# Key and value projection in split float16, and the masks' loads on another queue

## The chip, the cores and the metric

The kernel runs on one core of one Trainium2 chip. The metric is the device time of one execution in microseconds; lower is better. TensorE (PE) multiplies, VectorE (DVE), ScalarE (ACT) and GpSimd (POOL) work on tiles, SyncE (SP) issues transfers. ACT can issue transfers too; what an engine issues stands in its instruction stream, so an engine that waits for a transfer's buffer does nothing else meanwhile.

## The reference

Four blocks, each: cross attention of 256 tokens onto 4096 context rows of width 256 (16 heads of 16), a self-attention-like part, a feed-forward part. Only the context's projections matter here; for every layer l of the four

```
k = context @ Wk[l] + bk[l]      # 4096 x 256
v = context @ Wv[l] + bv[l]      # 4096 x 256
scores = q k^T / 4 (+ mask); out = softmax(scores) (* group_prob in layer 0) v; x = x + out @ Wo + bo
```

The context is the same for the four layers, so the kernel makes all keys and values ahead of the first block.

## The kernel before

`project_context` makes the four layers' keys and values; the rest of the kernel (four times `cross`, and the parts behind it) is not touched. A *key unit* is 128 key channels by 512 keys, 16 for each layer (2 halves of the channels by 8 chunks of the context); a *value unit* is 128 keys by 256 channels, 32 for each layer. The order is written out: the values of layer 0; the keys of layer 0; and for layers 1, 2 and 3 the keys and then the values. Each engine has its own loop over the same units, tied by counting semaphores.

A key unit goes through PE (`key_unit`, L510, two float32 products 128x128 by 512 columns, into one of four PSUM banks), ACT (`high`, L578, writes the float16 high part), DVE (L745, the low part: PSUM plus bias less the high part) and an SP transfer of 256 KB (L469) out of one of five slots of `kp`. The bank is free when DVE is done (`k_low`), the slot when the transfer has landed (`k_stored`). A value unit goes through PE (`value_unit`, L524, two float32 products of 256 columns) and DVE (L631, adds the bias into `vst`); eight units fill one of two slots of `vst`, which SP stores with 1 MB (L458).

While the values of layer 0 are made, the scale of the keys is found: ACT squares all weights (L589), PE sums them (`sum_weights`, L534), DVE reads the context's largest square (L644) and the sums (L652), PE sums again (`sum_squares`, L542), DVE works out a bound (L662 to L672), POOL takes its root (L776), DVE makes the scales, and POOL multiplies `wk` (L780). Then the first key unit can start. After key unit 4's predecessor (`EARLY = 4`) the query of layer 0 is projected in between (L230, L594, L314, L323, L331).

The mask is loaded as 32 pieces of 256 KB into two buffers `raw` (L610) and turned by POOL (L792). ACT issues these loads, eight behind the last key unit of each layer; the one for piece n waits until POOL has made piece n-2. ACT also issues the loads of `gT` (L614), two of 512 KB behind each layer's keys. In layer 2 DVE looks for tokens that see no key (`find_blind`, L711) and SP stores and reloads that row (L475, L462); in layer 3 DVE masks `gT` (`mask_factors`, L732 and L737). Behind the last mask piece POOL multiplies `qop` (L800).

Of the kernel before, what the change touches and what calls it, by code (L numbers as in the profile page):

```python
# [16 lines left out]
P = 128  # L17
D = 256
# [50 lines left out]
EXPONENT = 0x7F800000  # L69

# [303 lines left out]
def project_context(c):  # L374
# [10 lines left out]
    EARLY = 4  # L385
    K_BANKS, V_BANKS = (0, 1, 4, 5), (2, 3, 6, 7)
    X_BANK, Q_BANKS = 2, (3, 6)
    units = [(l, n) for l in range(LAYERS) for n in range(NK)]
    units_by = lambda slot, u: 16 * len([i for i in range(u) if i % VSLOTS == slot])
    stored_by = lambda slot, u: 16 * len([i for i in range(u) if i % SLOTS == slot])  # L390
    with ExitStack() as ctx:
# [3 lines left out]
        ctxT = sb("ctxT", [P, CT, KEYS], F32)  # L395
        wk = sb("wk", [P, LAYERS, CT, D], F32)
        wv = sb("wv", [P, CT, D], F32)
        bk = sb("bk", [P, LAYERS, CT], F32)
        bv = sb("bv", [P, 2, D], F32)
# [3 lines left out]
        wide = lambda first: c.gT[:, first:first + 8, :].rearrange("p (l t) n -> p l t n", l=LAYERS)  # L403
        wq_all, wk_square, wq_square = wide(0), wide(8), wide(16)
        ctx_square = sb("ctx_square", [P, NCHUNK], F32)
        squares = sb("squares", [P, 1 + 2 * LAYERS * CT], F32)
        totals = sb("totals", [P, 1 + 2 * LAYERS * CT], F32)
        quarter = sb("quarter", [P, LAYERS], F32)
        bound = sb("bound", [P, 4, LAYERS], F32)
        factor = sb("factor", [P, 4, LAYERS], F32)  # L410
        k_scale = sb("k_scale", [P, LAYERS], F32)
        per_layer = lambda a, at: a[:, 1 + at * LAYERS * CT:1 + (at + 1) * LAYERS * CT].rearrange("p (l t) -> p l t", l=LAYERS)
        block = ctx.enter_context(nc.Block())
        ctx_v = c.a["ctxT"].rearrange("(t p) k -> p t k", p=P)
        vout = c.vals.rearrange("l p (n h k e) -> l p n h k e", n=NV, h=H, k=VB)

        key_pieces = [m for b in (1, 0) for m in range(KT // 2) if m // 2 % 2 == b]

        def mask_piece(l, i):

            raw_i, n = raw[:, i % 2, :], PIECES * l + i
# [20 lines left out]
        def _(sp):  # L442
            def load_ctx(j):
                sp.dma_start(ctxT[:, :, j * CHUNK:(j + 1) * CHUNK], ctx_v[:, :, j * CHUNK:(j + 1) * CHUNK])\
                  .then_inc(S(f"ctx_loaded{j}"), 16)
# [3 lines left out]
            sp.dma_start(c.bq[:, :, :], c.a["bq4"]).then_inc(S("bias_loaded"), 16)  # L449
            sp.dma_start(c.wq[:, :, :], c.a["wq4"][0, :, :].rearrange("(t p) n -> p t n", p=P)).then_inc(S("wq_loaded"), 16)  # L450
            for j in (4, 1, 5, 2, 6, 3, 7):
                load_ctx(j)
# [12 lines left out]
            for l in range(LAYERS):  # L465
                for n in range(NK):
# [35 lines left out]
        def _(pe):  # L502
            def key_unit(l, n):
                u, mt, j = NK * l + n, n // NCHUNK, n % NCHUNK
                if n == 0:
                    pe.wait_ge(S("wk_scaled"), l + 1)
                if u >= 4:
                    pe.wait_ge(S("k_low"), u - 3)
                for ct in range(CT):
                    ins = pe.matmul(c.ps[:, K_BANKS[u % 4], :], wk[:, l, ct, mt * P:(mt + 1) * P],  # L510
                                    ctxT[:, ct, j * CHUNK:(j + 1) * CHUNK], start=(ct == 0), stop=(ct == CT - 1))
                ins.then_inc(S("k_psum"), 1)

            def value_unit(l, k):
                v = KT * l + k
                if k == 0:
                    pe.wait_ge(S("wv_loaded"), 16 * (l + 1))
# [3 lines left out]
                if l == 0:  # L521
                    pe.wait_ge(S(f"ctx_loaded{at // CHUNK}"), 16)
                for ct in range(CT):
                    ins = pe.matmul(c.ps[:, V_BANKS[v % 4], 0:D], ctxT[:, ct, at:at + P], wv[:, ct, :],  # L524
                                    start=(ct == 0), stop=(ct == CT - 1))
                ins.then_inc(S("v_psum"), 1)

            def sum_weights():
                pe.wait_ge(S("ones_set"), 1)
                pe.wait_ge(S("w_squared"), 2)  # L530
                for square, bank in ((wk_square, 0), (wq_square, 4)):
                    for two in range(2):
                        for ct in range(CT):
                            ins = pe.matmul(c.ps[:, bank + two, :], c.ones[:, 0:P], square[:, 2 * two:2 * two + 2, ct, :],  # L534
                                            start=(ct == 0), stop=(ct == CT - 1))
                ins.then_inc(S("w_summed"), 1)

            def sum_squares():
                pe.wait_ge(S("w_read"), 2)
                pe.wait_ge(S("b_squared"), 2)  # L540
                pe.wait_ge(S("ctx_read"), 1)
                pe.matmul(c.ps[:, 0, 0:1 + 2 * LAYERS * CT], c.ones[:, 0:P], squares[:, :], start=True, stop=True)\  # L542
                  .then_inc(S("squares_summed"), 1)

            for k in range(KT):
                value_unit(0, k)
                if k == 3 * GROUP - 1:
                    sum_weights()
                if k == 7 * GROUP - 1:
                    sum_squares()  # L550
            for l in range(LAYERS):
                for n in range(NK):
                    if NK * l + n == EARLY:
# [6 lines left out]
                        q.project(pe, S, Q_BANKS)  # L560
                    key_unit(l, n)
# [6 lines left out]
        def _(act):  # L568
            def load_values(l):
                act.dma_start(wv[:, :, :], c.a["wv4"][l, :, :].rearrange("(t p) n -> p t n", p=P)).then_inc(S("wv_loaded"), 16)  # L570
# [2369 lines left out]
```

## Time and profile before

| | |
|---|---|
| median of 3 runs | 1500.73 us (1494.08 to 1501.3) |
| the profiled execution: time, span | 1496.89 us, 1495.5 us |
| mean granted clock of TensorE | 0.944 of full |
| busy share of PE, DVE, ACT, POOL | 88%, 67%, 55%, 32% |
| `project_context` | from 0 to 278.5 us of the span |

A time in the trace is counted from the span's start. A matmul of float32 stands in the trace as two instructions. A granted clock of 1.00 is 2.4 GHz, one of 0.50 is 1.2 GHz, and a figure between is a stretch with both.

### The profile page before, as it was taken

To read this page: it belongs to the slowest core of one execution; us is meant where nothing else is said; L and a number is where in the kernel's file an instruction comes from. 1 tells how busy PE (TensorE), PEld (TensorE's weight loads), DVE (VectorE), ACT (ScalarE), POOL (GpSimd) and SP (SyncE) were. 2 spreads that over 40 slices of the span, in tenths; PEclk is the share of its full clock that TensorE was granted. 3 is DMA by queue.
4 is the path that set the end of the run, shared out by engine and by line. 5 is a ranking of instruction groups with operands and counts; after the bars stand their busy time and mean duration, and the time that the engine had idled before them with its cause. 6 is when DMAs were issued, how large, how long until landed. Compare 5 with 4: busy or idle time off the path is not lost. (4 is left out here: it accounts for less than half of the span.)

```text
span 1495.5 us, 29052 instructions
## 1 busy us (share of the span) xinstructions
PE 1319.7 (88%) x10626; PEld 664.7 (44%) x10626; DVE 1006.9 (67%) x2340; ACT 826.4 (55%) x1286; POOL 482.7 (32%) x681
## 2 busy tenths in 40 slices
PE   6879999699999988689999997869999896899987
PEld 4536576333333335523333355424444574344445
DVE  3524647699999944488888424369998144999942
ACT  1122202399999943048888824238888321678872
POOL 1321010489899870334444423111111000111100
PEclk9989999799999999969999999959999998799999
DMA  6266677311111302012113160622227201121400
GB/s 221 113 202 228 221 225 256 117 37 37 50 41 37 118 1 71 22 45 54 47 46 121 46 181 8 227 64 54 60 67 223 71 1 41 36 72 54 124 5 8
DMA packets 115731, 136.57 MB, mean 91 GB/s; under 512 B 13755, under 2 KB 96867, under 8 KB 113516
## 3 DMA queue, kind: packets, MB, share of 16 engines
q1 hardware_dynamic: 100486, 118.16, 25.9%
q10 hardware_dynamic: 15104, 16.56, 3.8%
q8 instruction: 85, 1.39, 0.4%
q14 instruction: 56, 0.46, 0.1%
HBM read 99.73 MB, written 34.90 MB: 90 GB/s over the span
## 5 line engine op out<-in xcount | busy, mean ns | idle before, releaser
L1193 ACT ACTIVATE prob_a<-ps 128x1024 f32<-128x1024 f32 x480 | 468.4, 1019 | 93.1 <-PE ps L1016 56.2
L998 PE MATMUL ps<-kop,qop 52*128 52x512 f16 x1024 | 302.0, 417 | 59.2 <-DMA qop<-qparts 20.5
L1217 DVE TENSOR_REDUCE best_a<-ps 128x1 f32<-128x512 f32 (+1 forms) x488 | 318.0, 710 | 26.4 <-PE ps L998 24.4
L1016 PE MATMUL ps<-qop,kop 52*128 52x256 f16 x2048 | 216.2, 278 | 6.2 <-ACT prob_a L1193 2.7
L1045 PE MATMUL ps<-prob_a,vop_a 128*32 128x256 f32 x3072 | 207.6, 390 | 4.7 <-issue 4.7
L1213 DVE CUSTOM_DVE_ANT_0 dump_a<-ps,neg_q 128x512 bf16<-128x512 f32 (+1 forms) x244 | 165.8, 715 | 40.6 <-PE ps L998 39.4
L998 PEld LDWEIGHTS ps<-kop,qop 52*128 52x128 f16 x1024 | 73.1, 95 | 242.0 <-DVE best_a L1217 97.2
L1331 POOL TENSOR_TENSOR used_a<-prob_a,gT 128x1024 f32<-128x1024 f32 x64 | 154.0, 2408 | 22.4 <-DVE used_a L1230 18.2
L578 ACT ACTIVATE kp<-ps,bk 128x512 f16<-128x512 f32 x64 | 43.7, 687 | 174.5 <-PE ps L510 159.8
L1016 PEld LDWEIGHTS ps<-qop,kop 52*128 52x128 f16 x2048 | 91.8, 95 | 103.5 <-issue 50.3
L1309 POOL TENSOR_SCALAR mrest_a<-nmax_a 128x2 f32<-128x2 f32 x64 | 27.8, 434 | 334.3 <-DVE nmax_a L1222 334.3
L510 PE MATMUL ps<-ctxT,wk 128*128 128x512 f32 x256 | 115.4, 612 | 12.9 <-DVE kp L745 10.2
L524 PE MATMUL ps<-wv,ctxT 128*128 128x256 f32 x512 | 117.6, 392 | 10.0 <-DMA wv<-in_wv 5.5
L1045 PEld LDWEIGHTS ps<-prob_a,vop_a 128*32 128x32 f32 x3072 | 84.5, 110 | 87.3 <-issue 53.6
L524 PEld LDWEIGHTS ps<-wv,ctxT 128*128 128x128 f32 x512 | 100.6, 197 | 27.3 <-DMA wv<-in_wv 5.5
L1361 POOL TENSOR_TENSOR prob_a<-prob_a,neg_k 128x1024 f32<-128x1024 f32 x32 | 68.4, 2139 | 109.5 <-ACT prob_a L1191 105.9
L1230 DVE SCALAR_TENSOR_TENSOR used_a<-prob_a,gT 128x1024 f32<-128x1024 f32 x64 | 95.7, 1495 | 6.5 <-ACT prob_a L1193 6.4
L1021 PE MATMUL ps<-neg_k,identb 128*128 128x512 bf16 x320 | 99.4, 393 | 0.0
L631 DVE TENSOR_TENSOR vst<-ps,bv 128x256 f32<-128x256 f32 x128 | 52.5, 423 | 64.4 <-PE ps L524 59.3
L745 DVE SCALAR_TENSOR_TENSOR kp<-ps,bk,kp 128x512 f16<-128x512 f32 x64 | 47.7, 750 | 64.7 <-ACT kp L578 64.7
L1133 ACT ACTIVATE qop<-ps 3x256 f16<-3x256 f32 x128 | 48.0, 375 | 75.6 <-PE ps L1071 72.8
L1045 PE MATMUL ps<-used_a,vop_a 128*32 128x256 f32 x1024 | 76.8, 392 | 10.6 <-DVE used_a L1230 5.6
(370 smaller groups left out, 1681.9 us busy)
## 6 DMA issues: line engine op xcount, KB each, us to landing
kop<-kparts SPq DMA_DIRECT2D x384, 64.0 KB, 2.3
vals<-vst SPq DMA_DIRECT2D x16, 1024.0 KB, 4.4
kparts<-kp SPq DMA_DIRECT2D x64, 256.0 KB, 2.4
vraw<-vals SPq DMA_DIRECT2D x64, 256.0 KB, 3.1
e_w<-in_e_w SPq DMA_DIRECT2D x4, 2048.0 KB, 12.1
z_w<-in_z_w SPq DMA_DIRECT2D x24, 256.0 KB, 6.9
ctxT<-in_ctxT SPq DMA_DIRECT2D x8, 512.0 KB, 12.2
raw<-in_mask ACTq DMA_DIRECT2D x16, 256.0 KB, 4.1
```

Of the source, the lines that this page charges most:

```text
L510: ins = pe.matmul(c.ps[:, K_BANKS[u % 4], :], wk[:, l, ct, mt * P:(mt + 1) * P], ctxT[:, ct, j * CHUNK:(j + 1) * CHUNK], start=(ct == 0), ...
L524: ins = pe.matmul(c.ps[:, V_BANKS[v % 4], 0:D], ctxT[:, ct, at:at + P], wv[:, ct, :], start=(ct == 0), stop=(ct == CT - 1))
L998: return pe.matmul(out, qop[rows, h, t * P:(t + 1) * P], kop[rows, h % UNROLL, first:first + CHUNK], start=True, stop=True)
L1016: ins = pe.matmul(st_bank(n)[:, j * NT:(j + 1) * NT], kop[rows, h % UNROLL, at:at + P], qop[rows, h, :], start=(j % 2 == 0), stop=(not add ...
L1021: ins = pe.matmul(st_bank(n)[:, j * NT:(j + 2) * NT], c.identb[:, :], c.neg_k[:, k:k + 2, :], start=False, stop=True)
L1045: ins = pe.matmul(sums_out[32 * j:32 * j + 32, :], vop[:, h % 2, g * GROUP + j, :], used[:, n % NP, j * NT:(j + 1) * NT], start=(g == 0 an ...
L1193: act.activation(prob[:, n % NP, :], st_bank(n), ACT.Exp, scale=1.0 / SCORE_UNIT).then_inc(S("exp_done"), 1)
L1213: dve.tensor_tensor_reduce(out=dump[:, k % 2, 0:width], in0=bank, in1=c.neg_q[:, t, j * CHUNK:j * CHUNK + width], scale=1.0, scalar=-3.0e3 ...
L1217: dve.tensor_reduce(out, bank, AX.X, ALU.max).then_inc(sem, 1)
L1230: dve.scalar_tensor_tensor(out=used[:, n % NP, :], in0=prob[:, n % NP, :], scalar=1.0, in1=c.gT[:, g * GROUP:(g + 1) * GROUP, :].rearrange ...
L1331: pool.tensor_tensor(used[:, n % NP, :], prob[:, n % NP, :], c.gT[:, g * GROUP:(g + 1) * GROUP, :].rearrange("p k q -> p (k q)"), ALU.mult)\
L1361: pool.tensor_tensor(prob[:, n % NP, :], prob[:, n % NP, :], seen(g).rearrange("p k q -> p (k q)"), ALU.mult)\
```

## The change

- The context and the weights of keys and values are scaled by powers of two and split in two float16 parts each. A product of float32 becomes three of float16 with one sum in PSUM: high by high, high by low, low by high. The values of layer 0 keep float32.
- The scale now needs sums of squares alone: ACT squares the context's 8 chunks and 12 weights with a sum along the row (20 instructions); the weights' sum on PE and the reads on DVE go. The values' bias and scale are put on in one DVE instruction.
- The parts: ACT writes the high part of a context chunk (128x1024), DVE the low part. Weights likewise (128x512), those of layers 1 to 3 in between the key units that `SPLIT_AT` lists.
- The mask's pieces are loaded by SP, one behind every second key unit; the query's clearing on POOL comes behind piece 25 and no more behind piece 31.
- All weights are loaded at the start; float32 context is staged in `gT`, the weights in `neg_k` and `vraw`, so `gT`'s loads of layer 0 wait for the last low part of the context.

```diff
+    SPLIT_AT = {9: ("wk", 1), 11: ("wv", 1), 14: ("wk", 2), 17: ("wv", 2), 20: ("wk", 3), 23: ("wv", 3)}
 ...
 # SP, behind key unit u
+                    if u % 2 == 1:
+                        load_mask(u // 2)
 ...
 # PE
+            PRODUCTS = [(ct, one, other) for ct in range(CT) for one, other in ((HIGH, HIGH), (HIGH, LOW), (LOW, HIGH))]
 ...
+                if u < NCHUNK:
+                    pe.wait_ge(S("ctx_low"), j + 1)
                 if u >= 4:
                     pe.wait_ge(S("k_low"), u - 3)
-                for ct in range(CT):
-                    ins = pe.matmul(c.ps[:, K_BANKS[u % 4], :], wk[:, l, ct, mt * P:(mt + 1) * P],
-                                    ctxT[:, ct, j * CHUNK:(j + 1) * CHUNK], start=(ct == 0), stop=(ct == CT - 1))
+                for i, (ct, w, k) in enumerate(PRODUCTS):
+                    ins = pe.matmul(c.ps[:, K_BANKS[u % 4], :], wkp[:, l, w, ct, mt * P:(mt + 1) * P],
+                                    ctxp[:, k, ct, chunk_cols(j)], start=(i == 0), stop=(i == len(PRODUCTS) - 1))
 ...
 # ACT
+            for i, j in enumerate(COME):
+                square_context(j)
+                if i < 4:
+                    square_weight(i, *weights[i])
+            for i in range(4, len(weights)):
+                square_weight(i, *weights[i])
+            act.wait_ge(S("squared"), NCHUNK + 3 * LAYERS)
+            act.wait_ge(S("scales"), 3)
+            weight_high("wk", 0)
+            for j in range(NCHUNK):
+                context_high(j)
 ...
                 high(u)
                 if n == NK - 1:
-                    for i in range(PIECES):
-                        piece = PIECES * l + i
-                        if piece >= 2:
-                            act.wait_ge(S("mask_made"), piece - 1)
-                        src, dst, _ = mask_piece(l, i)
-                        act.dma_start(dst, src).then_inc(S(f"mask_loaded{i % 2}"), 16)
 ...
 # DVE, key unit u
+                    if u < NCHUNK:
+                        context_low(u)
                     if u == EARLY:
                         q.low(dve, S, Q_BANKS)
+                    if u in SPLIT_AT:
+                        weight_low(*SPLIT_AT[u])
                     dve.wait_ge(S("k_high"), u + 1)
```

Where instructions stand, engine by engine. DVE before, from the first key unit on; `kp` is a key unit's low part, `qp` the query's, `vst` a value unit:

```order
L745 SCALAR_TENSOR_TENSOR kp<-ps,bk,kp 128x512 x4
L331 SCALAR_TENSOR_TENSOR qp<-ps,bq,qp 128x256 x2
L745 SCALAR_TENSOR_TENSOR kp<-ps,bk,kp 128x512 x28
L631 TENSOR_TENSOR vst<-ps,bv 128x16x16 x32
L745 SCALAR_TENSOR_TENSOR kp<-ps,bk,kp 128x512 x6
```

And DVE of the change at the same place, with the waits; `ctxp` is the low part of a context chunk, and `kv_k_high` counts ACT's high parts of key units:

```order
L744 SCALAR_TENSOR_TENSOR wkp<-neg_k,wk_scale,wkp 128x512 [waits kv_bk_scaled,kv_wk_high,kv_v_back,kv_scales]
L751 SCALAR_TENSOR_TENSOR ctxp<-gT,ctx_scale,ctxp 128x2x512 [waits kv_ctx_high]
L808 SCALAR_TENSOR_TENSOR kp<-ps,bk,kp 128x512 [waits kv_k_high]
L751 SCALAR_TENSOR_TENSOR ctxp<-gT,ctx_scale,ctxp 128x2x512 [waits kv_ctx_high]
L808 SCALAR_TENSOR_TENSOR kp<-ps,bk,kp 128x512 [waits kv_k_high]
```

The low parts of the context and of the key units now alternate, eight times, in DVE's one stream.

SP before, layers 0 and 1 (`kparts` is the store of a key unit, `vals` that of values):

```order
L295 DMA qop<-qparts 16x3072 x2
L469 DMA kparts<-kp 128x2x512 x23
L458 DMA vals<-vst 128x2048 x4
L469 DMA kparts<-kp 128x2x512
L275 DMA kop<-kparts 16x2048 x2
```

SP of the change, a stretch of the same layers, with the waits:

```order
L500 DMA kparts<-kp 128x2x512 [waits kv_k_low]
L483 DMA raw<-in_mask 128x512 [waits kv_mask_made]
L500 DMA kparts<-kp 128x2x512 [waits kv_k_low] x2
L483 DMA raw<-in_mask 128x512 [waits kv_mask_made]
L500 DMA kparts<-kp 128x2x512 [waits kv_k_low] x2
```

A mask piece, with its wait for POOL, now stands between the stores of key units.

## Rows read from the trace of the kernel before

**Rows 1.** Stretches: length; busy PE, PEld, DVE, ACT, POOL; clock; DMA share; GB/s.

```profile
0.00:60.10 60.10, 41.69 (x146) 30.60 (x147) 28.74 (x75) 5.10 (x3) 8.74 (x18) 0.94 0.50 182
60.10:95.70 35.60, 34.77 (x80) 16.11 (x81) 12.98 (x18) 12.43 (x19) 9.07 (x18) 0.91 0.49 156
95.70:109.70 14.00, 5.33 (x13) 2.09 (x11) 0.00 (x0) 0.04 (x1) 5.96 (x8) 0.79 0.66 208
109.70:135.00 25.30, 23.82 (x56) 11.32 (x57) 11.75 (x17) 10.73 (x16) 2.59 (x3) 0.91 0.56 191
135.00:161.60 26.60, 26.60 (x123) 23.20 (x123) 13.41 (x32) 0.00 (x0) 8.54 (x10) 1.00 0.72 248
161.60:190.10 28.50, 28.50 (x71) 13.28 (x70) 20.52 (x27) 10.99 (x16) 0.00 (x0) 1.00 0.74 234
190.10:221.20 31.10, 28.56 (x123) 24.30 (x123) 13.13 (x32) 0.00 (x0) 4.32 (x7) 0.95 0.79 217
221.20:249.70 28.50, 28.50 (x71) 13.29 (x70) 20.99 (x32) 10.99 (x16) 0.62 (x1) 1.00 0.73 234
249.70:278.50 28.80, 26.09 (x121) 22.62 (x120) 13.89 (x33) 0.00 (x0) 13.34 (x10) 0.99 0.72 252
```

**Rows 2.** Timeline: start us, duration us, then engine and instruction; PE.

```profile
36.87 13.98 PE L524 MATMUL ps<-wv,ctxT 128*128 128x256 f32 x64
...
73.40 27.63 PE L510 MATMUL ps<-ctxT,wk 128*128 128x512 f32 x64
```

**Rows 3.** A later line with 16-bit operands: timeline, and its weight loads (ns).

```profile
619.83 3.65 PE L868 MATMUL ps<-neg_k,idle 128*128 128x256 bf16 x32 [1.43 <-PEq L1651]
...
L868 PEld LDWEIGHTS ps<-neg_k,idle x32: 95/98/98, 619.8 to 623.1; 128*128 128x128 bf16 x32
```

**Rows 4.** Timeline of the stretch before the first key unit.

```profile
4.70 6.07 ACTq L585 DMA_DIRECT2D gT<-in_wq  x4
...
11.24 10.80 PE L524 MATMUL ps<-wv,ctxT 128*128 128x256 f32 x40 [1.96 <-DMA ctxT<-in_ctxT]
...
53.41 0.37 PE L542 MATMUL ps<-squares,ones 128*128 128x17 f32 x2 [2.56 <-DVE squares L698]
...
60.10 10.21 PE L510 MATMUL ps<-ctxT,wk 128*128 128x512 f32 x16 [2.72 <-POOL wk L780]
```

**Rows 5.** Timeline: one key unit behind PE (its matmuls start at 73.40).

```profile
75.32 0.69 ACT L578 ACTIVATE kp<-ps,bk 128x512 f16<-128x512 f32 x1 [1.24 <-PE ps L510]
...
76.04 0.75 DVE L745 SCALAR_TENSOR_TENSOR kp<-ps,bk,kp 128x512 f16<-128x512 f32 x1 [1.45 <-ACT kp L578]
```

**Rows 6.** Durations (ns, min/median/max) of the nearest forms, from later stages.

```profile
L1230 DVE SCALAR_TENSOR_TENSOR used_a<-prob_a,gT x64: 1215/1507/3324, 302.2 to 550.5; 128x1024 f32<-128x1024 f32 x64
L1193 ACT ACTIVATE prob_a<-ps x480: 999/1019/1112, 299.2 to 1446.5; 128x1024 f32<-128x1024 f32 x160
L1146 ACT ACTIVATE used_a<-used_a,best_a x16: 706/722/722, 280.9 to 298.4; 128x512 f32<-128x512 f32 x16
```

**Rows 7.** Two stretches with a sparse PE, columns as in the first group.

```profile
285.00:295.00 10.00, 5.24 (x20) 1.05 (x20) 9.96 (x20) 7.35 (x21) 4.34 (x8) 0.50 0.20 61
1265.00:1270.00 5.00, 2.82 (x10) 0.47 (x10) 5.00 (x5) 0.00 (x0) 0.00 (x0) 0.50 0.03 10
```

**Rows 8.** Timeline of ACT between the keys of layers 0 and 1.

```profile
99.17 10.39 ACTq L610 DMA_DIRECT2D raw<-in_mask  x6
109.66 0.69 ACT L578 ACTIVATE kp<-ps,bk 128x512 f16<-128x512 f32 x1 [14.77 <-POOL neg_q L792]
```

**Rows 9.** Mask pieces: issue to landing; and a stretch of layer 2's keys.

```profile
DMA to landing us min/median/max: 2.6/4.1/16.8
...
170.00:180.00 10.00, 10.00 (x25) 4.50 (x24) 8.58 (x11) 3.85 (x6) 0.00 (x0) 1.00 0.68 214
```

**Rows 10.** Timeline of DVE in the values of layer 2.

```profile
207.91 1.42 DVE L631 TENSOR_TENSOR vst<-ps,bv 128x256 f32<-128x256 f32 x4 [5.05 <-DMA vals<-vst]
```

**Rows 11.** Timeline of POOL at the end of the stage.

```profile
270.39 8.00 POOL L800 TENSOR_TENSOR qop<-qop,sighted 128x4096 f16<-128x4096 f16 x1
```

More of the change, by code:

```diff
@@ L521, in value_unit, with sum_squares @@
                 if l == 0:
+                    if k == 0:
+                        pe.wait_ge(S("wv_in0"), 16)
                     pe.wait_ge(S(f"ctx_loaded{at // CHUNK}"), 16)
[L523 to L525 removed]
+                    for ct in range(CT):
+                        ins = pe.matmul(c.ps[:, V_BANKS[v % 4], 0:D], ctx32[:, ct, at:at + P], w32["wv"][:, 0, ct, :],
+                                        start=(ct == 0), stop=(ct == CT - 1))
+                else:
+                    for i, (ct, one, w) in enumerate(PRODUCTS):
+                        ins = pe.matmul(c.ps[:, V_BANKS[v % 4], 0:D], ctxp[:, one, ct, at:at + P], wvp[:, l, w, ct, :],
+                                        start=(i == 0), stop=(i == len(PRODUCTS) - 1))
                 ins.then_inc(S("v_psum"), 1)
[L528 removed]
+            def sum_squares():
                 pe.wait_ge(S("ones_set"), 1)
[L530 to L539, printed above, removed]
                 pe.wait_ge(S("b_squared"), 2)
[L541 to L542 removed]
+                pe.wait_ge(S("squared"), NCHUNK + 3 * LAYERS)
+                pe.matmul(c.ps[:, 0, 0:SUMS], c.ones[:, 0:P], squares[:, :], start=True, stop=True)\
                   .then_inc(S("squares_summed"), 1)
             for k in range(KT):
+                if k == SUM_AT:
+                    sum_squares()
                 value_unit(0, k)
[L547 to L550, printed above, removed]
             for l in range(LAYERS):
@@ L622, in stage_values @@
             def stage_values(l, first, n):
[L624 to L625 removed]
+                if first == 0 and l == 0:
+                    dve.wait_ge(S("bv_loaded"), 16 * LAYERS)
                 for k in range(first, first + n):
@@ L655, in _ @@
+                    if l == 0:
+                        dve.tensor_tensor(vst[:, b % VSLOTS, :, k % VB, :], found, bias, ALU.add).then_inc(S("v_staged"), 1)
+                    else:
+                        dve.scalar_tensor_tensor(out=vst[:, b % VSLOTS, :, k % VB, :], in0=found, scalar=v_back[:, l:l + 1],
+                                                 in1=bias, op0=ALU.mult, op1=ALU.add).then_inc(S("v_staged"), 1)
             link = Chain(dve, S("bound_step"))
-            k_bound, q_bound, k_bias, q_bias = (bound[:, i, :] for i in range(4))
@@ new lines, in _ @@
+            pool.wait_ge(S("exponents_set"), 2)
+            pool.wait_ge(S("base"), 1)
+            pool.tensor_tensor(root[:, :], base[:, :], exponents[:, :], ALU.pow).then_inc(S("root"), 1)
+            pool.wait_ge(S("wq_loaded"), 16)
+            pool.wait_ge(S("q_scale"), 1)
+            pool.tensor_scalar(c.wq[:, :, :], c.wq[:, :, :], c.q_scale[:, 0:1], None, ALU.mult).then_inc(S("wq_scaled"), 1)
+            fill_constants(c, pool, S)
+            pool.wait_ge(S("squared"), NCHUNK + 3 * LAYERS)
@@ new lines, in _ @@
+            for n in range(LAYERS * PIECES):
+                pool.wait_ge(S(f"mask_loaded{n % 2}"), 16 * (n // 2 + 1))
+                if n == 2 * PIECES:
+                    pool.wait_ge(S("wk_low"), LAYERS)
+                    pool.wait_ge(S("wv_low"), LAYERS - 1)
+                _, src, dst = mask_piece(n)
+                pool.tensor_scalar(dst, src, -1.0, -NEG, ALU.add, ALU.mult).then_inc(S("mask_made"), 1)
+                pool.wait_ge(S("mask_made"), n + 1)
+                if n < 2 * PIECES and n % 4 == 1:
+                    u = n // 4
+                    pool.memset(c.ops.kop[:, u, :], MAX_UNIT).then_inc(S("kop_ones"), 1)
+                    pool.wait_ge(S("kop_ones"), u + 1)
+                if n == CLEAR_AT:
+                    pool.wait_ge(S("blind_loaded"), 16)
+                    pool.tensor_scalar(sighted[:, :], blind, -1.0, 1.0, ALU.mult, ALU.add).then_inc(S("sighted"), 1)
+                    pool.wait_ge(S("sighted"), 1)
+                    pool.wait_ge(c.ops.S("q_first"), Q_DONE)
+                    pool.wait_ge(c.ops.S("q_rest"), Q_DONE)
+                    pool.tensor_tensor(c.qop[:, :, :], c.qop[:, :, :], sighted[:, :].unsqueeze(1).to_broadcast((P, H, NT)), ALU.mult)\
+                        .then_inc(S("sighted"), 1)
```

265 lines of the change are left out of this document (135 added, 130 removed).

## The prediction

> **What bounds the kernel now.** I read the page first, then the stretches of the projection one by one, then the timeline at their joints. The page says that PE is busy for 88% of the span; but only the projection is changed, so only the first 278.5 us are looked at. [rows 1] gives its stages: the prelude with the values of layer 0 (0 to 60.1), the keys of layer 0 (to 95.7), a hole (to 109.7), the keys and values of layer 1 (to 135.0 and 161.6), of layer 2 (190.1, 221.2) and of layer 3 (249.7, 278.5). In the keys and values of layers 1 to 3 PE is busy from end to end at the full clock, while DVE has 13 to 21 us of work in stretches of 27 to 31: PE is the bound there. [rows 2] gives its pace: 64 instructions are 16 units, so a key unit takes 27.63/16 = 1.73 us, a value unit 13.98/16 = 0.87 (0.86 without the drain at the end).
>
> Two stretches aren't bound by PE. In the hole PE is busy for 5.33 of 14.0 us: ACT issues six mask loads over 10.39 us, each of which waits for POOL, and its next key unit starts at 109.66 after 14.77 us of idling that POOL ends [rows 8]; behind it the four PSUM banks are full. In the prelude a chain sets the end: weights landed, squared, summed, the context read, the second sum at 53.41, the scales, first key unit at 60.10 [rows 4].
>
> **Part by part.** Each stage now and then, from the same boundaries.
>
> *16-bit products.* Six for each unit instead of four float32 instructions of twice the time. The nearest row is L868: 32 matmuls of 128x128 by 256 columns of bf16 in 3.65 us less a drain of some 0.2, that is 0.108 each, and each with its own weight load of 0.098 [rows 3]. So the load lies beside the matmul, a value unit is 6 x 0.108 = 0.65 us and a key unit, at twice the columns, 1.30 (estimates). The other bound has the load exposed: 0.108 + 0.098. I take the row's own pace, since it holds the loads already.
> The Trainium skill ("TensorE: Matmul & The Clock Gate", section "The mechanism") speaks against this: a weight load runs beside a matmul only where the row groups differ. By that rule a value unit would take 6 x 0.206 = 1.24 us, more than before. The trace disagrees, with 0.108 for full arrays in a row.
>
> *Values, layers 1 to 3.* 32 x 0.65 = 20.7 us for each layer. DVE's instruction gets a multiplication, which I cost at nothing: 13.4 us for 32 [rows 1] stays below 20.7 even at half as much again. Layer 1: 26.6 to 20.7, -5.9. Layer 2 had a wait of 5.05 us for a slot of `vst` [rows 10], behind the tiny writes of the blind row. They stay; the mask pieces that shared the queues with them go; the slot is wanted 1.7 us sooner. I put the wait at 3.3: 31.1 to 24.0, -7.1. Layer 3: from 249.7 to the stage's end at 278.5, of which the last 2 us are POOL's `qop` product (270.39 + 8.00) [rows 11], now done much earlier: 28.8 to 21.3, -7.5.
>
> *Keys of layer 1, with the hole.* From 95.7 to 135.0, 39.3 us. The masks leave ACT's stream, so the hole goes. What is late next is the loop of the mask pieces in SP's stream: piece n waits for piece n-2, which was issued four units earlier. Landing takes 4.1 us in the middle and POOL and the issue about 1.1, so the loop wants 5.2 us for four units, 1.30 each [rows 9]: just at PE's pace. While SP waits, the key stores queue behind it, and ACT waits for those when five slots are full. DMA: a store of 256 KB and half a mask piece for each 1.30 us are 300 GB/s; layer 2's keys ran at 214 GB/s with a share of 0.68 [rows 9], so full is about 315. That is near the limit. I take 1.35 us: 21.6, so -17.7 (12 of it the hole).
>
> *Keys of layer 2.* DVE has 20.52 us of work in it [rows 1], 12 of them the low parts (16 x 0.75 [rows 5]) and the rest eight reads of the mask, so that eight units cost DVE 1.8 us each and are its bound. 8 x 1.8 + 8 x 1.3 + 0.6 at the joint = 25.4: -3.1. *Keys of layer 3.* DVE 21 us, PE 20.8, both with little room, `kop` loads on the same queues; POOL's 8 us product now stands in front of piece 26, and SP's wait for it holds the stores of units 58 on; I cost that at 3. 16 x 1.4 + 0.6 + 3 = 26.0: -2.5.
>
> *Prelude.* The weights' sum on PE and the context's reads on DVE go. The new chain is ACT's: 17 issues instead of 10, of which the last four took 6.07 us before [rows 4], so that they end at about 14; the table load; then 8 squares of 128x1024 (1.02 plus the read of the sum, 1.15) and 12 of 128x512 (0.72 in a row) [rows 6] = 17.8 us, to 33. PE gets its second context chunk at 11.24 [rows 4]; 22 units of 0.86 behind that it is at unit 24, at 30, and waits there. The sum, the bound, POOL's root and the scales took 53.4 to 60.1 before; again some 6 us, in which PE finishes the last eight values by 41 (by 47 if the wait halves its clock). Then the low parts of `wk` and of the first chunk on DVE. First key unit at 45 (43.5 to 51): -15.1.
>
> *Keys of layer 0: here time is lost.* DVE's stream reads: low part of chunk u, low part of key unit u, low part of chunk u+1. The second waits for ACT's high part, this for PE's key unit u, and this for the low part of chunk u. Nothing overlaps any more; four units used to be in flight, now it is one. For each of the first eight units the chain is: chunk's low part 1.22 (the least of the nearest row, L1230; its middle is 1.51) [rows 6], PE 1.30 at the full clock, 0.21 to ACT, 0.72 to DVE, 0.67 [rows 5], 0.07 of semaphores: 4.2 us instead of 1.73. And PE would be busy for only 31% of that. In the trace it stands at 0.50 of the clock where it is as sparse: 5.24 of 10 us, 2.82 of 5 [rows 7]. At that clock the key unit takes 2.6 and its drain a little longer, so the period is 5.6 to 5.7 us with PE busy for 46%. I take the half clock. From the first key unit to the ninth: 7 x 5.67 + 2.6 + 1.5 for the query's projection, which lies in the same chain = 43.8 us, against 80.3 - 60.1 = 20.2 before: +23.6. The other eight units: two still at the slow clock, six at 1.3, some low parts of weights: 15 us, as before.
>
> **Sum.** -15.1 + 23.6 + 0 - 17.7 - 5.9 - 3.1 - 7.1 - 2.5 - 7.5 = -35.3 us, and nothing behind the projection changes but its start: 1496.9 - 35.3 = 1461.6 by the profiled execution, 1465.4 by the median, which is 3.8 above it. I say 1463.
>
> **The rivals.**
> (a) *Full clock in the eight serial units.* The period is then 4.2: 7 x 4.2 + 1.3 + 1.5 = 32.2 instead of 43.8, and the two units behind it are fast as well: 14 us less, 1449. For it: the clock was full in most of the projection. Against it: [rows 7], where it stays low at a greater share than these units have. Chance 0.13.
> (b) *The mask loop or the DMA queues set the pace of the keys.* At a landing of 6 us, which the row's spread of 2.6 to 16.8 allows [rows 9], the loop is 7.1 us for four units, 1.78 each: layer 1 +6.9, layer 3 +6, half a layer 0 +3.5, and the slots of `vst` +3: 1482. For it: 300 of some 315 GB/s, and stores and pieces in one queue. Against it: POOL has room, five slots cover 6.5 us. Chance 0.22.
> (c) *Weight loads of 16 bits aren't hidden.* Then each of the products costs 0.098 more: 336 in key units and 576 in value units, 912 x 0.098 = 89 us: 1552, slower than before. It decides from 35/912 = 0.039 us of exposed load on. Against it: [rows 3], where full arrays of 16 bits ran at 0.108 with a load each. What could still speak for it: these few matmuls are the only ones of that form, and both of their operands were at rest, while here PSUM sums over six. Chance 0.03.
> The Trainium skill's rule that is named above would bring this case about.
> (d) *The gain is eaten.* A wait that I don't see, of some 35 us in all, such as mask pieces that land behind whole value stores: within 0.5% of 1500.7. Chance 0.04.
> The forecast itself, the serial units at the slow clock and keys near PE's pace, has 0.58 and a range of its own of 1453 to 1473.
>
> **How the numbers follow.** The likeliest gives 1463. The range takes in (a) and (b) with their bounds and leaves (c) and (d) outside: 1446 to 1483. A measurement of this kernel tells about 0.5% (7.5 us) from no change; all cases but (c) and (d) are faster by more: faster 0.93, within 0.5% 0.04, slower 0.03.
>
> **What would show it.** In the trace after: first key unit at about 45; the starts of the first eight low parts 5.6 us apart (4.2 for (a)) and DVE idle for more than half of that, the waits ended by ACT; a granted clock of 0.5 there; no hole between the keys of layers 0 and 1; value units 0.65 us and key units 1.3 apart in layer 1; the stage's end at 243. Wrong it would be by key units 1.7 us apart with DVE or ACT waiting for `kp`'s stores (b), or value units over 1 us (c).

## The result, and the profile after

| | median | runs |
|---|---|---|
| before | 1499.72 us | 4, 1494.08 to 1501.3 |
| changed | 1482.69 us | 4, 1479.2 to 1483.3 |

The ratio is 0.989 (95% interval 0.986 to 0.992): 17 us faster, where the sum of the prediction was 35. The profiled execution took 1479.2 us, its span is 1478.0.

The stretches of the changed kernel, with the columns of [rows 1]: the prelude, the eight first key units of layer 0, its other eight, then keys and values of layers 1, 2 and 3 in turn, and last all that lies behind the projection.

```profile
0.00:49.00 49.00, 35.89 (x131) 29.32 (x132) 20.02 (x63) 24.49 (x49) 12.86 (x32) 0.93 0.69 247
...
49.00:91.00 42.00, 24.70 (x65) 9.54 (x66) 14.79 (x17) 8.64 (x13) 3.66 (x4) 0.63 0.25 82
91.00:104.20 13.20, 13.20 (x62) 5.88 (x60) 8.33 (x12) 7.66 (x12) 1.30 (x3) 1.00 0.84 256
104.20:127.40 23.20, 20.33 (x103) 9.58 (x102) 13.50 (x20) 12.23 (x19) 8.54 (x10) 1.00 0.99 314
127.40:148.40 21.00, 19.16 (x171) 16.68 (x172) 14.61 (x33) 0.00 (x0) 3.66 (x4) 1.00 0.70 257
148.40:173.40 25.00, 23.36 (x118) 11.08 (x116) 20.50 (x28) 10.94 (x16) 3.09 (x5) 1.00 0.89 286
173.40:201.70 28.30, 21.77 (x172) 18.02 (x173) 14.74 (x32) 0.00 (x0) 1.85 (x3) 0.88 0.79 207
201.70:231.50 29.80, 24.39 (x109) 11.04 (x108) 27.15 (x33) 11.00 (x16) 13.38 (x8) 0.89 0.73 237
...
254.50:1478.00 1223.50, 1081.13 (x9828) 510.66 (x9828) 871.35 (x2077) 776.54 (x1216) 427.42 (x608) 0.94 0.22 65
```

The projection ends at 254.5 instead of 278.8, 24.3 us earlier (both at VectorE's first instruction of the next stage). The rest of the kernel took 1223.5 us; in the profiled execution of before it took 1495.5 - 278.8 = 1216.7. So there are two shortfalls against the sum of 35.3: 11 us within the projection, and 7 us behind it, where the change touches nothing.

VectorE's timeline in the first key units of layer 0 (start, duration, instruction, idle time before it and who ended it):

```profile
52.40 0.75 DVE L808 SCALAR_TENSOR_TENSOR kp<-ps,bk,kp 128x512 f16<-128x512 f32 x1 [3.58 <-ACT kp L633]
53.06 1.27 DVE L751 SCALAR_TENSOR_TENSOR ctxp<-gT,ctx_scale,ctxp 128x1024 f16<-128x1024 f32 x1
57.89 0.75 DVE L808 SCALAR_TENSOR_TENSOR kp<-ps,bk,kp 128x512 f16<-128x512 f32 x1 [3.56 <-ACT kp L633]
58.56 1.28 DVE L751 SCALAR_TENSOR_TENSOR ctxp<-gT,ctx_scale,ctxp 128x1024 f16<-128x1024 f32 x1
```

The period is 5.49 us, and VectorE idles 3.56 of it: the serial chain of the prediction. Two of the seven periods are only 4.8 us and the one with the query in it is 6.8; over the whole stretch the granted clock is 0.63 and not 0.50, so some of it ran at 2.4 GHz. Its timeline in the values of layer 2:

```profile
177.34 0.48 DVE L693 SCALAR_TENSOR_TENSOR vst<-ps,v_back,bv 128x256 f32<-128x256 f32 x1 [0.17 <-PE ps L568]
177.99 0.48 DVE L693 SCALAR_TENSOR_TENSOR vst<-ps,v_back,bv 128x256 f32<-128x256 f32 x1 [0.17 <-PE ps L568]
...
190.04 1.66 DVE L693 SCALAR_TENSOR_TENSOR vst<-ps,v_back,bv 128x256 f32<-128x256 f32 x4 [7.63 <-DMA vals<-vst]
```

Value units are 0.65 us apart, six products with their weight loads. But the wait for a slot of `vst`, 5.05 before [rows 10], is now 7.63. And VectorE, then GpSimd, in the keys of layer 3:

```profile
216.43 7.58 DVE L796 TENSOR_TENSOR gT<-gT,att 128x512 f32<-128x512 f32 x1
...
225.85 0.68 DVE L796 TENSOR_TENSOR gT<-gT,att 128x512 f32<-128x512 f32 x1
```

```profile
215.46 7.99 POOL L865 TENSOR_TENSOR qop<-qop,sighted 128x4096 f16<-128x4096 f16 x1
```

One instruction of VectorE takes 7.58 us where its twin takes 0.68, and ends half a microsecond after GpSimd's long product. This product is the one of [rows 11], placed earlier.

### The profile page after: what moved, and what is told of

It is laid out like the page before. It is cut to its first block and busy times, and to the rows that moved or that the text cites. A ratio compares the mean times of both kernels' runs of the same rounds, so it can differ in the third digit from the quotient of the medians.

```text
span 1478.0 us, 29726 instructions
## 1 busy us (share of the span) xinstructions
PE 1283.8 (87%) x10930; PEld 638.9 (43%) x10930; DVE 1020.6 (69%) x2341; ACT 851.6 (58%) x1339; POOL 477.5 (32%) x678
## 5 line engine op out<-in xcount | busy, mean ns | idle before, releaser
L1392 POOL TENSOR_TENSOR used_a<-prob_a,gT 128x1024 f32<-128x1024 f32 x64 | 152.9, 2389 | 25.4 <-DVE used_a L1291 19.4
L1370 POOL TENSOR_SCALAR mrest_a<-nmax_a 128x2 f32<-128x2 f32 x64 | 27.8, 434 | 334.2 <-DVE nmax_a L1283 334.2
L548 PE MATMUL ps<-ctxp,wkp 128*128 128x512 f16 x384 | 96.2, 411 | 27.9 <-DVE ctxp L751 19.1
L633 ACT ACTIVATE kp<-ps,bk 128x512 f16<-128x512 f32 x64 | 43.7, 687 | 127.7 <-PE ps L548 104.3
L1207 ACT ACTIVATE below_a<-below_a,best_a 128x512 f32<-128x512 f32 x112 | 80.3, 717 | 8.5 <-DVE best_a L1270 8.2
L229 POOL TENSOR_TENSOR rstd<-var,minus_half 128x2 f32<-128x2 f32 x11 | 7.8, 713 | 235.9 <-DVE var L219 226.1
L1270 DVE CUSTOM_DVE_ANT_0 dump_a<-ps,neg_q 128x512 bf16<-128x512 f32 x112 | 76.5, 683 | 1.8 <-PE ps L1059 1.8
```

What stands on the lines that cost most here:

```text
L548: ins = pe.matmul(c.ps[:, K_BANKS[u % 4], :], wkp[:, l, w, ct, mt * P:(mt + 1) * P], ctxp[:, k, ct, chunk_cols(j)], start=(i == 0), stop=( ...
L1207: act.activation(lowered, lowered, ACT.Exp, scale=-1.0, bias=best[:, h % 2, at:at + 1], accum_out=part[:, h % 4, t, own.index(j):own.index ...
L1270: dve.tensor_tensor_reduce(out=dump[:, 0, 0:width] if lowered is None else lowered, in0=bank, in1=c.neg_q[:, t, j * CHUNK:j * CHUNK + widt ...
L1392: pool.tensor_tensor(used[:, n % NP, :], prob[:, n % NP, :], c.gT[:, g * GROUP:(g + 1) * GROUP, :].rearrange("p k q -> p (k q)"), ALU.mult)\
```

## The experiments

Each was timed in a round together with the kernel before, on one chip. The ratios are against that; the kernel before took 1499.7 us in the round of the changed kernel and 1500.5 (experiments 1 to 4), 1501.4 (5 to 8) and 1497.7 (9 to 11) in the others. Where an edit starts from the changed kernel, its time is to be held against 1482.7 us, with some 3 us of doubt for the round, and the end of its projection against 254.5. The end is read from one trace of each kernel; two traces of the kernel before differ by 5.9 us there (experiment 8).

**1. The low part of the context one chunk ahead.**

```diff
-                    if u < NCHUNK:
-                        context_low(u)
+                    if u == 0:
+                        context_low(0)
+                    if u + 1 < NCHUNK:
+                        context_low(u + 1)
```

> The changed kernel with one edit: VectorE makes the low part of the context's chunk u+1 ahead of the low key part of unit u, not behind it. Our theory: the first eight key units are a chain VectorE 1.28, TensorE 2.6, ScalarE 0.7, VectorE 0.7 us (period 5.5 us at half clock), and nothing else holds them. With the low part one chunk ahead TensorE at half clock (2.6 us a unit) is the longest step; seven periods come to 18 to 21 us instead of 38.4, layer 0's key units end some 15 to 19 us earlier, and the whole is 1464 to 1468 us against 1483 of the changed kernel. Rival: the transfers set the pace once the chain is broken (DMA share is 0.84 to 0.99 in the units behind it), the gain is given back in layers 0 and 1, and the whole is 1475 to 1483.

Measured: 1459.35 us, ratio 0.972 (0.968 to 0.977). A stretch of the first units, and VectorE in it:

```profile
51.00:69.00 18.00, 13.58 (x62) 6.36 (x61) 14.16 (x16) 6.91 (x12) 3.59 (x4) 1.00 0.50 160
```

```profile
51.54 0.75 DVE L810 SCALAR_TENSOR_TENSOR kp<-ps,bk,kp 128x512 f16<-128x512 f32 x1 [2.49 <-ACT kp L633]
52.21 1.28 DVE L751 SCALAR_TENSOR_TENSOR ctxp<-gT,ctx_scale,ctxp 128x1024 f16<-128x1024 f32 x1
53.40 0.75 DVE L810 SCALAR_TENSOR_TENSOR kp<-ps,bk,kp 128x512 f16<-128x512 f32 x1
```

The period falls to between 1.86 and 2.37 us where the query does not stand between, TensorE is granted the full clock, and layer 0's key units end at 81.7 instead of 104.2. Nothing of that 22 is given back later: the projection ends at 232.5. The chain was worth about what the prediction put on it (+23.6), clock included, and it was the order of two calls in VectorE's stream that made it.

**2. GpSimd's product behind the last piece.**

```diff
-CLEAR_AT = 25
+CLEAR_AT = 31
```

> The changed kernel with GpSimd's product over the whole query operand (8.0 us) behind the last mask piece instead of behind piece 25, so that it lies beside the value units of layer 3, where VectorE reads PSUM, and not beside VectorE's products of two SBUF operands in layer 3's key units. Our theory: VectorE's product of 7.58 us falls back to about 0.7, the stage of keys 3 from 29.8 to 22 to 24 us, the additions beside the product stay at 0.42 us, and the whole is 6 to 8 us faster than the changed kernel (1475 to 1477). Rival: the stage's key units wait for SyncE's transfers and not for VectorE, and the whole stays at 1481 to 1484; or the late product now ends behind the value units and the next stage waits for it, 1480 and more.

Measured: 1471.55 us, ratio 0.982 (0.976 to 0.987). The eight products of VectorE (ns, min/median/max), the stretch of the keys of layer 3, and GpSimd's product:

```profile
L796 DVE TENSOR_TENSOR gT<-gT,att x8: 675/681/1127, 204.7 to 224.5; 128x512 f32<-128x512 f32 x8
```

```profile
201.30:224.60 23.30, 22.77 (x118) 11.27 (x116) 20.75 (x32) 10.91 (x16) 3.23 (x5) 1.00 0.94 304
```

```profile
235.02 8.01 POOL L865 TENSOR_TENSOR qop<-qop,sighted 128x4096 f16<-128x4096 f16 x1
```

The stretch takes 23.3 us instead of 29.8, and the projection ends at 246.5, 8.0 earlier. While the product runs from 235.0 to 243.0, VectorE stages value units, each reading PSUM, in 0.48 us as ever. So it is not GpSimd's work as such that stops VectorE, but the two together where VectorE's operands both lie in SBUF.

The edit also takes the product out of the way of mask piece 26, for which SyncE waits. The changed kernel's own waits in the keys of layer 3 (201 to 232 us; total, times, longest) tell the two apart:

```profile
PE ps L548 <- DVE kp L808: 5.4, 1, 5.4
...
ACT kp L633 <- DMA kparts<-kp: 2.2, 2, 1.4
```

TensorE waited 5.4 us at one place for VectorE, and ScalarE 2.2 in all for key stores. What SyncE's wait would cost with VectorE free, no run shows.

The trace of the kernel before has the same collision, in a later stage: VectorE and GpSimd there both multiply with SBUF operands, `prob_a` by `gT`.

```profile
323.46 1.22 DVE L1230 SCALAR_TENSOR_TENSOR used_a<-prob_a,gT 128x1024 f32<-128x1024 f32 x1
...
540.02 3.32 DVE L1230 SCALAR_TENSOR_TENSOR used_a<-prob_a,gT 128x1024 f32<-128x1024 f32 x1 [2.30 <-ACT prob_a L1193]
```

```profile
539.91 2.35 POOL L1331 TENSOR_TENSOR used_a<-prob_a,gT 128x1024 f32<-128x1024 f32 x1
```

VectorE's instruction takes 1.22 us where no long product of GpSimd lies beside it. The one at 540.02 takes 3.32 and ends 1.08 us after GpSimd's. So the spread of this line in [rows 6], 1215 to 3324 ns, had the price in it. The Trainium skill ("GPSIMD Engine Reference", section "1. Specifications") says that GpSimd's interfaces to SBUF are shared with VectorE and contend with its instructions that have two inputs in SBUF; the traces agree, and show the price: VectorE's instruction waits for the whole of GpSimd's.

**3. Filler products in the serial units.** Six matmuls on constant tiles ahead of key units 1 to 7; nothing is left out.

```diff
+                    if 0 < NK * l + n < NCHUNK:
+                        pe.wait_ge(S("placed"), 2)
+                        pe.wait_ge(S("later_filled"), 4)
+                        keep_warm(c, pe, 6)
                     key_unit(l, n)
```

> The changed kernel with six matrix products of 512 columns on constant tiles into a free bank ahead of each of key units 1 to 7 (added work, nothing left out), in the time in which TensorE waits for the context's low part. Our theory: the half clock of the serial units comes from TensorE's idle time, the filler removes it, the products of a unit take 1.3 us instead of 2.6, the period goes from 5.5 to 4.2 us and layer 0's key units end 5 to 8 us earlier: 1475 to 1478. Rival: the clock stays at half, the filler at 0.43 us a product (2.6 us) lies in the wait of 2.8 us and nothing moves, 1481 to 1484, or it ends late and each unit is longer.

Measured: 1476.63 us (1470.2 to 1481.8), ratio 0.983 (0.977 to 0.988). TensorE's timeline:

```profile
52.59 2.74 PE L548 MATMUL ps<-ctxp,wkp 128*128 128x512 f16 x6 [2.94 <-DVE ctxp L755]
55.12 1.80 PE L245 MATMUL ps<-idle,identb 128*128 128x512 bf16 x6
58.09 1.47 PE L548 MATMUL ps<-ctxp,wkp 128*128 128x512 f16 x6 [1.17 <-DVE ctxp L755]
```

The clock rises behind the first filler, the six products of a unit take 1.47 us instead of 2.74, and the period is 4.2 (low parts at 56.08 and 60.31): our first rival's figure, reached by added work. So the half clock is worth 1.3 us of a period, and the rest of the chain stays. The projection ends at 245.3, 9.2 earlier. The median shows 6.1 of that; experiment 8 looks at the rest.

**4. The masks' move alone**, on the kernel before: the loop of mask loads leaves ScalarE's stream, and `load_mask(u // 2)` stands behind every second key store in SyncE's. Products stay float32.

> The kernel before with the mask change alone: the mask pieces are started by SyncE behind every second key unit as in the changed kernel; float32 products and everything else as before. Our theory: the 14.8 us in which ScalarE issues masks at the end of layer 0's key units go away, the key stages of layers 1 to 3, which are TensorE's at four float32 products a unit, have room for the masks' transfers, and the whole is 10 to 14 us faster than before (1486 to 1490). So the mask change makes most of the measured 17 us. Rival: the masks slow the key stages as much as they gave (SyncE waits, DMA), 1496 to 1502.

Measured: 1485.74 us, ratio 0.989 (0.983 to 0.994), as large a gain against its own round (14.8 us) as that of the whole change, within the intervals. The keys of layer 1, and of layer 2:

```profile
98.00:125.50 27.50, 27.50 (x69) 12.85 (x68) 11.96 (x18) 10.89 (x16) 10.57 (x12) 1.00 0.92 295
152.10:180.60 28.50, 28.50 (x71) 13.25 (x71) 20.49 (x28) 11.00 (x16) 3.72 (x6) 1.00 0.90 282
```

The hole is gone, and the masks' transfers cost the key stages of this float32 form nothing: TensorE is busy from end to end, and layer 2's keys take 28.5 us as in [rows 1], at a DMA share of 0.90 where it was 0.74.

**5. The split alone**: the changed kernel with the mask loads back in ScalarE's stream, and GpSimd's product behind the last of them.

> The changed kernel with the mask pieces started by ScalarE at the end of each layer's key units, as in the kernel before (and GpSimd's product behind the last piece, as before): the float16 split alone. Theory: the parts of the change add up. The mask change alone gave 14 us; with the late product the changed kernel took 1471.6; so this takes 1471.6 + 14 = 1484 to 1488, with a ScalarE hole of 10 to 15 us at the end of layer 0's key units. Rival: the masks' transfers in the key stages cost the float16 form time that they do not cost the float32 form (DMA share is 0.99 in keys 1), so with the masks elsewhere the key stages shrink below those of the changed kernel and the whole is 1475 to 1481.

Measured: 1492.88 us over 10 runs (1484.0 to 1496.6), ratio 0.994 (0.991 to 0.996), slower than either theory said. ScalarE at the end of layer 0's keys:

```profile
104.14 10.70 ACTq L665 DMA_DIRECT2D raw<-in_mask  x6
114.94 0.69 ACT L624 ACTIVATE kp<-ps,bk 128x512 f16<-128x512 f32 x1 [14.14 <-POOL neg_q L851]
```

The hole is back at its full size. But this kernel has a loss of its own, at the end of the projection: VectorE, then GpSimd.

```profile
251.11 0.48 DVE L691 SCALAR_TENSOR_TENSOR vst<-ps,v_back,bv 128x256 f32<-128x256 f32 x1 [0.17 <-PE ps L559]
263.51 0.09 DVE L1307 MEMSET best_a<- 128x32 f32 x1 [11.91 <-PEq L404]
```

```profile
253.24 1.32 POOL L851 TENSOR_SCALAR neg_k<-raw 128x512 bf16<-128x512 int32 x2 [5.00 <-DMA raw<-in_maskT]
255.14 7.97 POOL L863 TENSOR_TENSOR qop<-qop,sighted 128x4096 f16<-128x4096 f16 x1
```

The last value is staged at 251.6, and the next stage starts 11.9 us later, behind the last mask pieces and GpSimd's product. In the kernel before, whose values are slower, the same product ends 2 us behind the last value. Neither theory had this; it can account for the time being above both. The parts measured by themselves are 15 us for the masks and 8.5 for the split, 23.5 together, against 17 for both. They don't add simply: the split alone has this end, which the masks' move takes away, and only the whole change has GpSimd's collision (8 us in the trace of experiment 2).

**6. Edits 1 and 2 together.**

> The changed kernel with both edits of before: low part of the context one chunk ahead, GpSimd's product last. Theory: both gains add, -22 to -24 and -7 to -11 from 1483: 1449 to 1454. Rival: with the first stage shorter the later ones wait for transfers and the sum is cut: 1456 to 1460.

Measured: 1448.93 us, ratio 0.968 (0.963 to 0.972). The projection ends at 226.0; the 22.0 and 8.0 of the single edits predict 224.5. They add, within 1.5 us.

**7. A third slot for value stores.**

```diff
-    NV, VSLOTS = V_UNITS, 2
+    NV, VSLOTS = V_UNITS, 3
```

> The changed kernel with three value staging slots instead of two (the tile for the product's factor lies in the query parts' tile to make room). Theory: the waits of VectorE for a value store (2.9 us in layer 1, 7.6 in layer 2, 2.9 in layer 3) come from a free slot missing while a store of 1 MB lies behind the key stages' transfers; with a third slot the waits fall to 0 to 3 us in all and the half clock behind the wait of layer 2 goes too: 8 to 12 us faster than the changed kernel, 1471 to 1475. Rival: the DMA engines are the limit, the stores land no sooner, and the same time is waited in the next key stage, where the key stores wait behind them: 1480 to 1484.

Measured: 1470.33 us, ratio 0.982 (0.978 to 0.987). VectorE's waits for value stores in layers 1 to 3 (us in total, times, longest), first in the changed kernel:

```profile
DVE vst L693 <- DMA vals<-vst: 13.5, 3, 7.6
```

and with three slots, with the stretch of layer 2's values:

```profile
DVE vst L693 <- DMA vals<-vst: 3.3, 1, 3.3
```

```profile
170.60:192.00 21.40, 19.17 (x171) 16.66 (x172) 14.62 (x33) 0.00 (x0) 1.85 (x3) 1.00 0.99 264
```

Layer 2's values take 21.4 us instead of 28.3, and the next keys are not slower for it. The projection ends at 242.1, 12.4 earlier, which is also what the median shows. This kernel also repeats experiment 2's finding: the product of VectorE beside GpSimd's takes 7.28 us in it.

**8. The kernel before, unchanged, for a second trace.**

> The kernel before, unchanged, for a second trace of it. Theory: how long the part behind the projection takes differs between executions of one kernel with the time for which TensorE is at half clock; the first trace (1216.7 us behind the projection, 1495.5 in all) was of the faster kind, and this one is 1218 to 1226 us behind the projection with more half clock there; the projection itself takes the same 278.8 us within 1. Rival: the part behind the projection is 1216 to 1218 again, and what was lost there in the changed kernel comes from the change.

Measured: 1495.08 us, span 1493.7. All that lies behind the projection, in the first trace of before, in the second, in the kernel of experiment 3 and in that of experiment 6:

```profile
278.80:1495.50 1216.70, 1075.81 (x9828) 507.89 (x9828) 871.43 (x2077) 776.06 (x1216) 429.40 (x608) 0.94 0.23 64
```

```profile
272.90:1493.70 1220.80, 1065.90 (x9753) 508.92 (x9828) 872.30 (x2077) 776.05 (x1216) 430.14 (x608) 0.94 0.22 64
```

```profile
245.30:1478.60 1233.30, 1091.56 (x9828) 513.35 (x9828) 871.24 (x2077) 776.25 (x1216) 426.35 (x608) 0.93 0.22 64
```

```profile
226.00:1444.80 1218.80, 1063.34 (x9753) 508.06 (x9828) 875.34 (x2077) 776.35 (x1216) 429.06 (x608) 0.94 0.22 65
```

The same instructions, with the same busy time on VectorE, ScalarE and GpSimd, take 1217 to 1233 us. The trace also lists the stretches in which the clock was at 0.50. Behind the projection they add up to 138.1, 145.2, 180.4 and 140.1 us in these four, and to 152.3 in the changed kernel (1223.5 us). Over all thirteen traces at hand a straight line fits, 0.39 us of time for each microsecond at the lower level, with no trace further off than 2.5 us. So what was lost behind the projection goes with the clock, and both vary between executions of one kernel. No run changes the clock there and nothing else.

The first half of the expectation came true: 1220.8 us behind the projection, with more half clock. The second half failed: the projection is 5.9 us shorter in this trace (272.9). Its first low key part comes 2.4 us sooner (62.4 against 64.8), and layer 2's values take 27.8 us and not 31.1, with a wait of 3.45 instead of 5.05 for the slot and no stretch at half clock behind it. Our sum was made against an execution with a slow projection.

**9. Eight slots for key parts instead of five** (`SLOTS = 8`).

> The changed kernel with eight staging slots for key parts instead of five. Theory: ScalarE's waits for a key store (22.9 us in the key stages) are the transfers' own pace in layer 1 (DMA share 0.99 at 314 GB/s) and beside VectorE's in layers 2 and 3; more slots only put the wait off: the stage of keys 1 falls by 0 to 2 us, the others by less than 1, the whole is 1480 to 1484. Rival (our second rival's limit by slots): the landing times of 4.4 to 12.6 us with five slots set the pace, and eight give 5 to 9 us: 1474 to 1478.

Measured: 1478.78 us, ratio 0.985 (0.980 to 0.990), between the two. The keys of layer 1, and ScalarE's waits for key stores in layers 1 to 3:

```profile
101.30:122.00 20.70, 20.70 (x105) 10.08 (x104) 13.62 (x20) 12.42 (x19) 8.21 (x9) 1.00 0.99 326
```

```profile
ACT kp L633 <- DMA kparts<-kp: 3.7, 5, 1.0
```

In the changed kernel these waits come to 20.1 us. With more slots layer 1's keys take 20.7 us instead of 23.2, as many as TensorE needs, although the DMA share was 0.99 before too. That was more than our theory allowed. But VectorE's waits for value stores grow from 13.5 to 16.1 us, layer 1's values take 24.8 us instead of 21.0, and the projection ends at 253.9: what the key stage gains, the value stage loses. The median is 3.9 us below that of the changed kernel; the 0.6 us of the projection in the trace do not bear this out, and it is within the doubt for the round.

**10. Three weight loads issued by SyncE, not by ScalarE** (`load_weight` of `wv`, layers 1 to 3).

> The changed kernel with the loads of the value weights of layers 1 to 3 started by SyncE behind the query weights, not by ScalarE, whose first Square then waits for 4.45 us of issuing less. Theory: our prelude came out 4.0 us late because ScalarE issued its 17 loads until 18.9 us and not 14; so here the squares end 3 to 4 us earlier, the first key unit starts at 45 to 46 instead of 49.0, and the whole is 3 to 4 us faster than the changed kernel (1478 to 1480). Rival: the squares wait for the landing of the context's chunks, or the value units at half clock end at 46 to 47 anyway and hold VectorE: the first key unit at 48 to 49 and no change.

Measured: 1479.15 us, ratio 0.988 (0.982 to 0.993), not to be told from the changed kernel; the projection ends at 254.8. The first key unit starts at 47.3 instead of 49.0. ScalarE (first row) does start 4.5 us sooner; VectorE (second) then waits for a value store:

```profile
14.36 1.28 ACT L620 ACT_TABLE_LOAD   x1 [14.36 <-issue]
```

```profile
30.15 1.42 DVE L694 TENSOR_TENSOR vst<-ps,bv 128x256 f32<-128x256 f32 x4 [6.51 <-DMA vals<-vst]
```

The store of layer 0's first values now lies behind those loads. Both have to go: in experiment 11 the first low key part starts at 46.1 us, against 52.4 in the changed kernel, 51.6 here and 51.8 with the third value slot alone. The first key units start at 41.7, 49.0, 47.3 and 48.6. Experiment 11 also has the full clock from 30 to 40 us, where the changed kernel has 0.50 from 36.5 to 42; the two gains are not separated.

**11. Edits 1, 2, 7 and 10 together.**

> All of it together: low part ahead, product last, three value slots, value weights loaded by SyncE. Theory: from the 1449 of the first two, 8 to 13 us less for the value slots and 0 to 4 for the loads: 1432 to 1441, key stages of 23 to 25 us and value stages of 21 to 22.5 in layers 1 to 3. Rival: without the waits for the value stores the transfers back up into the key stages, which are at a DMA share of 0.92 to 0.98, and the whole is 1442 to 1449.

Measured: 1441.21 us (1434.4 to 1442.2), ratio 0.960 (0.955 to 0.965), the fastest of all. Keys and values of layer 2 and keys of layer 3, and all behind the projection:

```profile
121.30:146.10 24.80, 23.20 (x118) 11.07 (x116) 20.39 (x28) 10.95 (x16) 3.10 (x5) 1.00 0.92 291
146.10:167.20 21.10, 19.23 (x172) 16.72 (x173) 14.68 (x33) 0.00 (x0) 1.86 (x3) 1.00 1.04 272
167.20:189.60 22.40, 22.40 (x116) 11.20 (x115) 20.07 (x32) 11.00 (x16) 4.14 (x5) 1.00 0.92 308
...
210.80:1439.00 1228.20, 1072.93 (x9753) 511.95 (x9828) 875.73 (x2077) 776.62 (x1216) 429.88 (x608) 0.93 0.22 64
```

The stages are as expected or up to 1.5 us shorter, and the projection ends at 210.8, 43.7 earlier than in the changed kernel. The time lies at the upper edge of the forecast. In the profiled execution the part behind took 1228.2 us, of them 163.3 at half clock; in the changed kernel it took 1223.5.

## Why the prediction was wrong

The prediction said 1463 us and 35 us of gain; measured are 1482.7 and 17. That the time lies in the range, 0.3 us from its end at 1483, is luck: that end was drawn for rival (b), 1482, and most of what was lost was not (b)'s. Term by term, from the traces. The first two rows and their differences are points in time; the 4.0 of the first is made up for by the second. The others are lengths, and they are what is missing.

| step | forecast, us | changed, us | difference |
|---|---|---|---|
| first key unit | 45 | 49.0 | +4.0 |
| end of layer 0's keys | 104.2 | 104.2 | 0 |
| keys 1 | 21.6 | 23.2 | +1.6 |
| values 1 | 20.7 | 21.0 | +0.3 |
| keys 2 | 25.4 | 25.0 | -0.4 |
| values 2 | 24.0 | 28.3 | +4.3 |
| keys 3 | 26.0 | 29.8 | +3.8 |
| values 3 and end | 21.3 | 23.0 | +1.7 |
| behind | 0 | | +6.8 |

- **Right:** the pace of the 16-bit products with their weight loads hidden (value units 0.65 us apart, rival (c) dead); the serial chain and its half clock (0.63 over the stretch, period 5.49 where 5.67 was said; experiment 3 takes the half clock away and leaves the chain, experiment 1 breaks the chain, and the clock rises with it); the hole (experiment 4); the length of keys 2. That VectorE bounds keys 2 was not tested by itself; without masks (experiment 5) and with eight key slots (9) it takes 24.6 us instead of 25.0.
- **First key unit, mis-sized:** "so that they end at about 14". ScalarE's issues ended at 18.9, the last three in 4.45 us. Behind the squares, the last eight values ran from 36.5 to 46.5 us, with the clock at 0.50 until 42, and VectorE reached the key units' first parts only behind them, at 46.9. The prediction had named this ("by 47 if the wait halves its clock") and did not take it into its 45. The half clock lengthened the serial stretch by less than was forecast, which made up for the 4.0 at 104.2. Taking the three issues away alone brings 1.7 us of the 4.0 back, and a value store then lands late (experiment 10).
- **Values 2, mis-sized:** "I put the wait at 3.3". It was 7.6. The prediction had the slot wanted sooner, but said that the mask pieces "that shared the queues with them go". They did not all go: SyncE issued one at 172.2 us and one at 175.7, just ahead of the store at 177.2. The store of 1 MB is started 5 us before its slot is wanted again and landed 12.8 us after its start. The third slot removes it (experiment 7). What among the transfers ahead makes the landing long was not separated.
- **Keys 3, the step that failed:** the 8 us product "now stands in front of piece 26, and SP's wait for it holds the stores"; "I cost that at 3". The stage without the product takes 23.3 us, as the other terms said (23.0); with it 29.8, so the product cost 6.5 and not 3. And the price was on VectorE, not in SyncE's stream: two instructions on SBUF operands excluded each other (experiment 2), 6.9 us in one instruction. In the kernel before, this product of GpSimd lay beside additions that read PSUM and cost VectorE nothing. But the collision stood in the same trace, at 540 us, and in the largest value of a line that the prediction took the least value of (L1230, [rows 6]).
- **Rival (b)** came true in small: keys 1 ran at a DMA share of 0.99 and 1.45 us a unit. The mask loop was not what held it: with the same loop and eight key slots the stage takes 20.7 us (experiment 9). The key slots were, for 2.5 us, and the value stage behind gave that back.
- **"Nothing behind the projection changes", failed in time though not in work:** -24.3 became -17.5 between the two spans. The prediction put this term at nothing and gave no width for it. Experiment 8 shows this part of the same kernel at 1216.7 and at 1220.8, with more half clock in the latter. That the changed kernel's start is shifted may matter for which stretches get the lower clock; no run here separates that from chance.
- **The baseline:** terms were read from one execution, whose projection was 5.9 us longer than in the second trace. Against the second, the projection gained 272.9 - 254.5 = 18.4 us, and of the 31.1 us that the forecast started from in values 2, 3.3 were that execution's own.

## What to carry to other kernels

When a preparation step for unit u+1 stands behind the finishing step of unit u in one engine's stream, the pipeline is one unit deep: put it one ahead, before counting the gain of faster products. Before moving a long GpSimd instruction, list what VectorE does beside its new place: here instructions with two SBUF operands waited for all of it, and ones that read PSUM did not. Where a line's largest duration is far above its least, look what the other engines did beside the long ones, before taking the least as the price. A faster engine wants its staging slots sooner, so redo the count of slots against the longest landing seen, and not the median.

## What was not expected of the hardware

- VectorE's product of two SBUF tiles took 7.58 and 7.28 us beside GpSimd's product of 8 us, up to 1.13 beside the turning of a mask piece (0.62 us), and 0.68 with nothing beside it; its instructions that read PSUM kept their 0.48 us.
- A DMA share of 0.99 did not mean that the transfers were the limit: with more slots the same units ran at 20.7 us instead of 23.2, at 326 GB/s instead of 314.
- The same instructions behind the projection took 1217 to 1233 us, in step with the time that TensorE spent at 1.2 GHz.
